# Gated cross-attention on one core: the instructions of a head in another order, with every step's place written out

## The reference

```python
def _L0_xattn_ref(latents, context, Wq, Wk, Wv, Wo, q_norm_w, k_norm_w):
    kv = jnp.concatenate([context, latents], axis=1)
    q = (latents @ Wq).reshape(bsz, q_len, HEADS, HEAD_DIM).transpose(0, 2, 1, 3)
    k = (kv @ Wk).reshape(bsz, kv_len, KV_HEADS, HEAD_DIM).transpose(0, 2, 1, 3)
    v = (kv @ Wv).reshape(bsz, kv_len, KV_HEADS, HEAD_DIM).transpose(0, 2, 1, 3)
    q = rms_norm(q, q_norm_w)
    k = rms_norm(k, k_norm_w)
    scores = jnp.einsum('bhgqd,bhkd->bhgqk', qg, k) * scale
    probs = jax.nn.softmax(scores.astype(jnp.float32), axis=-1).astype(q.dtype)
    out = jnp.einsum('bhgqk,bhkd->bhgqd', probs, v)
    return out @ Wo
x = x + jnp.tanh(g_xattn[0]) * _L0_xattn_ref(_layernorm(x), ctx_4096, ...)
x = x + jnp.tanh(g_ffn[0]) * _L0_ffn_ref(_layernorm(x), ...)
```

## Time and profile before

| what | before |
|---|---|
| median of 3 runs | 3681.51 us (3675.87 to 3684.28) |
| the profiled execution, its own time | 3666.57 us |
| its span in the profile | 3664.7 us |
| PE busy | 3162.6 us, 86% |
| DVE busy | 2476.6 us, 68% |
| ACT busy | 2036.9 us, 56% |
| POOL busy | 1343.4 us, 37% |
| mean granted TensorE clock | 0.955 |

### The profile page before, as it was taken

The page is one execution under the profiler, slowest core; times in us unless marked ns, Lnnn a source line. Parts: engine busy times, 40 slices in busy tenths (PEclk is TensorE's granted clock), DMA queues, the critical chain, the costliest instruction groups (busy, mean ns, idle before and its releaser), DMA issues. The chain is left out here.

```text
span 3664.7 us, 52293 instructions
## 1 busy us (share of the span) xinstructions
PE 3162.6 (86%) x14906; PEld 2518.2 (69%) x14906; DVE 2476.6 (68%) x3316; ACT 2036.9 (56%) x2899; POOL 1343.4 (37%) x791
## 2 busy tenths in 40 slices
PE   7978888888888888888888888888888888599699
PEld 5856677767667677766677776767776777377477
DVE  6854767777857777777677777676777677632666
ACT  3435666666656666665566666666666666431211
POOL 2321444444524444444244444443444444400000
PEclk9989999999999999999999999999999999799799
DMA  7870000000210000102000100020100000243410
GB/s 241 262 232 30 30 29 29 29 29 29 68 39 29 29 29 31 34 23 80 24 29 31 34 29 29 23 79 27 35 29 29 29 29 18 81 149 97 148 35 18
DMA packets 183908, 210.88 MB, mean 58 GB/s; under 512 B 10964, under 2 KB 125652, under 8 KB 182760
## 3 DMA queue, kind: packets, MB, share of 16 engines
q1 hardware_dynamic: 179016, 196.27, 16.6%
q0 software_dynamic: 2176, 8.39, 0.7%
q10 hardware_dynamic: 2592, 4.72, 0.4%
HBM read 140.14 MB, written 69.21 MB: 57 GB/s over the span
## 5 line engine op out<-in xcount | busy, mean ns | idle before, releaser
L745 ACT ACTIVATE att_sc<-att_pqk,att_rk 128x512 f32<-128x512 f32 (+1 forms) x960 | 661.8, 689 | 865.6 <-PE att_pqk L653 844.2
L867 POOL TENSOR_TENSOR att_sm<-att_sm,att_sc 128x1024 f32<-128x1024 f32 (+1 forms) x384 | 849.4, 2212 | 754.3 <-DVE att_pr L818 753.3
L673 PE MATMUL att_ppv<-att_pr,att_V 128*128 128x512 f32 (+1 forms) x2880 | 896.0, 421 | 127.9 <-ACT att_oraw L760 85.4
L653 PE MATMUL att_pqk<-att_q,att_kT 128*128 128x512 f32 (+1 forms) x2880 | 855.0, 407 | 7.9 <-issue 5.9
L614 PE MATMUL att_pkv<-att_ctxT,att_wkv 128*128 128x512 f32 (+1 forms) x3072 | 772.0, 384 | 102.5 <-DVE att_V L847 102.3
L614 PEld LDWEIGHTS att_pkv<-att_ctxT,att_wkv 128*128 128x128 f32 x3072 | 565.2, 193 | 234.4 <-DVE att_V L847 113.0
L673 PEld LDWEIGHTS att_ppv<-att_pr,att_V 128*128 128x128 f32 (+1 forms) x2880 | 524.9, 196 | 259.9 <-ACT att_oraw L760 103.4
L818 DVE TENSOR_TENSOR att_pr<-att_sc,att_pr 128x1024 fp32r<-128x1024 f32 (+1 forms) x512 | 628.1, 1227 | 109.0 <-ACT att_pr L756 108.7
L801 DVE TENSOR_TENSOR att_pmx<-att_pmx,att_sc 128x512 f32<-128x512 f32 x768 | 533.0, 694 | 237.8 <-ACT att_sc L745 232.6
L653 PEld LDWEIGHTS att_pqk<-att_q,att_kT 128*128 128x128 f32 (+1 forms) x2880 | 542.0, 191 | 146.4 <-ACT att_sc L745 8.1
L812 DVE TENSOR_TENSOR att_sc<-att_sc,att_pmax 128x1024 f32<-128x1024 f32 (+1 forms) x512 | 584.6, 1142 | 0.0
(11 more groups left out here) (130 smaller groups left out, 2738.4 us busy)
## 6 DMA issues: line engine op xcount, KB each, us to landing
q_scr<-pre_qT SPq DMA_DIRECT2D x128, 256.0 KB, 3.6
att_wkv<-kv_scr SPq DMA_DIRECT2D x64, 512.0 KB, 4.1
att_q<-q_scr SPq DMA_DIRECT2D x64, 512.0 KB, 4.1
o_scr<-att_on SPq DMA_DIRECT2D x64, 256.0 KB, 2.0
out_oraw<-o_scr SPq DMA_DIRECT2D x64, 256.0 KB, 4.6
att_sc<-in_ctx SPq DMA_DIRECT2D x16, 768.0 KB, 4.7
pre_wq_raw<-in_L_xattn_Wq SPq DMA_DIRECT2D x8, 1024.0 KB, 7.0
kv_scr<-pre_kv SPq DMA_DIRECT2D x8, 1024.0 KB, 7.5
```

Source lines behind the costliest of these rows:

```text
L653: mm = pe.matmul(pqk[0:m, (h * NT + t) % 2], kT[:, kp, t * P:t * P + m], q[:, qp, h], start=(i == 0), stop=(i == 2))
L673: mm = pe.matmul(ppv[:], V[0:m, vp, t], pr[0:m, pp, (t // 2) % NP, t % 2], start=(t == 0 and i == 0), stop=(t == NT - 1 and i == 2))
L745: act.activation(sc[0:m, h, t], pqk[0:m, s % 2], ACT.Copy, scale=rk[0:m, t:t + 1]).then_inc(sc_ok, 1)
L867: pool.tensor_tensor(sm[0:m, 0:w], sm[0:m, 0:w], sc[0:m, h, i:i + w], ALU.add).then_inc(sum_ok, w)
```

## The change

The step list gets a new form: the distances between steps, which were formulas (`p - 4.3`, `e + 1.59`, `k + i * 0.82`), become a table in which every kind of step has a place, for the two halves and for each chunk of keys and values apart. No step is added or removed, and no instruction, wait or buffer in the steps is changed. Lines after the table stand 3 lower than before.

```diff
--- before.py
+++ after.py
@@ -433,34 +433,37 @@
 
 
         LAG = 24
-        steps = []
+        TILE = dict(copy=0.39, pv=24.2, sub=19.6, exp=20.8, hi=21.6, lo=22.5, sum=23.0, max=1.78)
+        END = dict(mt=(2.49, 2.89),
+                   red=(2.9, 3.1),
+                   mb=(4.7, 5.1),
+                   oraw=(23.2, 23.2),
+                   fold=(23.8, 22.5),
+                   dt=(24.77, 24.07),
+                   dred=(25.03, 24.73),
+                   db=(26.66, 27.36),
+                   on=(30.31, 45.01),
+                   st=(28.31, 28.31),
+                   ldq=(-29.9, -29.9))
+        CHUNK = (dict(k=(-11.56, -11.5, -11.28), v=(1.44, 1.92, 2.0), khi=-11.46, klo=-9.93, kn=-6.16, var=-6.26, pow=-7.26, vhi=2.74, vt=12.5, vthi=13.36, vtlo=16.04),
+                 dict(k=(-7.48, -7.26, -6.8), v=(3.2, 7.72, 9.42), khi=-7.06, klo=-6.93, kn=-1.36, var=-2.36, pow=1.34, vhi=9.74, vt=16.8, vthi=17.26, vtlo=16.94),
+                 dict(k=(-5.79, -5.21, -4.47), v=(9.44, 13.2, 14.34), khi=-4.27, klo=-2.84, kn=0.23, var=-0.67, pow=5.33, vhi=15.24, vt=21.3, vthi=21.06, vtlo=21.64),
+                 dict(k=(-1.08, -0.66, -0.4), v=(17.82, 19.2, 19.34), khi=-0.06, klo=-0.63, kn=1.84, var=4.24, pow=8.84, vhi=19.74, vt=26.5, vthi=26.06, vtlo=27.24))
+        LOADS = dict(ldwk=-31.6, ldwv=-16.8)
+        steps = [(place, what, 0, 0) for what, place in LOADS.items()]
         for h in range(NH):
             for t in range(NT):
                 p = h * NT + t
-                steps += [(p, "qk", h, t), (p + 0.39, "copy", h, t), (p + LAG, "pv", h, t)]
+                steps += [(p, "qk", h, t), (p + TILE["copy"], "copy", h, t), (p + TILE["pv"], "pv", h, t)]
+                if t >= 1:
+                    steps += [(p + TILE["max"], "max", h, t)]
             for g, (t, z) in enumerate(GR):
-                p = h * NT + t + LAG
-                steps += [(p - 4.3, "sub", h, g), (p - 3.2, "exp", h, g), (p - 2.4, "hi", h, g), (p - 1.6, "lo", h, g)]
-                if g >= 1:
-                    steps += [(p - 0.9, "sum", h, g)]
-            for t in range(1, NT):
-                steps += [(h * NT + t + 1.18, "max", h, t)]
-            e = (h + 1) * NT
-            steps += [(e + 1.59, "mt", h, 0), (e + 1.7, "red", h, 0), (e + 3, "mb", h, 0)]
-            f = e + LAG
-            steps += [(f - 0.6, "oraw", h, 0), (f - 0.5, "fold", h, 0), (f + 1.17, "dt", h, 0), (f + 1.83, "dred", h, 0),
-                      (f + 3.76, "db", h, 0), (f + 4.21, "on", h, 0), (f + 4.31, "st", h, 0)]
-            steps += [(h * NT - NT + .1, "ldq", h, 0)]
-
-        for c, (k, v, vt) in enumerate(((-12.7, 1, 12.6), (-9, 6, 16.6), (-3.21, 13, 20.6), (-1.5, 17.5, 24.6))):
-            for i in range(PARTS):
-                steps += [(k + i * 0.82, "k", i, c), (v + i * 0.82, "v", i, c)]
-            k, v = k + (PARTS - 1) * 0.82, v + (PARTS - 1) * 0.82
-            steps += [(k + 0.9, "khi", 0, c), (k + 1.03, "klo", 0, c), (k + 3.5, "kn", 0, c),
-                      (k + 3.6, "var", 0, c), (k + 3.7, "pow", 0, c)]
-            steps += [(v + 0.9, "vhi", 0, c)]
-            steps += [(vt, "vt", 0, c), (vt + 0.76, "vthi", 0, c), (vt + 1.64, "vtlo", 0, c)]
-        steps += [(-28, "ldwk", 0, 0), (-10.4, "ldwv", 0, 0)]
+                p = h * NT + t
+                steps += [(p + TILE[what], what, h, g) for what in ("sub", "exp", "hi", "lo", "sum") if g >= 1 or what != "sum"]
+            steps += [((h + 1) * NT + place[h], what, h, 0) for what, place in END.items()]
+        for c, places in enumerate(CHUNK):
+            for what, place in places.items():
+                steps += [(p, what, i, c) for i, p in enumerate(place)] if what in ("k", "v") else [(place, what, 0, c)]
         steps.sort()
```

## The result

The changed kernel takes 3226.81 us (median of 4 runs, 3225.14 to 3228.32), the kernel before 3680.64 (4 runs, 3675.87 to 3684.28). The ratio is 0.8768, with a 95% interval of 0.8752 to 0.8783. The forecast was 3340, its range 3290 to 3460: the sign and the cause held, the gain was a third larger than foreseen, and the time lies 63 us under the range.

The account below looks back on a forecast made before the run. PE was taken as the bound: 74.67 us of work plus 10.63 of waits a round. Terms of -286, -29, -20 and -6 sum to -341; from the median 3681.5 that gives 3340 us, range 3290 to 3460.

Parts of the forecast that it names:

- the sign: Whole kernel: faster by more than 0.2%, about 8 us; chance 0.94, against 0.02 for within and 0.04 for slower.
- the cause: PE in the rounds: its waits behind chains just begun on PE go, about 0.45 us of 10.63 staying.
- the eight waits: PE waits in a steady round, for `sub`, `vhi`, `oraw` (twice), `vtlo` (twice), `klo` and `lo`: 10.63 us in all.
- The one foreseen to stay: `pv` of the next half waiting for `oraw`, with `exp` ahead on ACT: 0.45 us left a round.
- 24 rounds: Steady rounds of the four stretches: 75.5 us each, 1812 in place of 2097.75 us, so -286.
- The clock term: Half-clock spells in the 24 rounds, taken as gone with the waits; worth 50 us if all stayed.
- Last and first rounds and boundaries: Rest of each batch's last round -29, first rounds -20, three boundaries -6 us.
- the four waits of the earlier trace: PE waits in the first round of each batch, 7.1 us; 5 taken as going, -20 over the batches.
- The row that spoke against the change: `lo` between two batches held by POOL's `sum`, 2.56 against 1.221 us; expected holds of a few tenths, within margins.
- Rival 1: DVE becomes the bound: 14 full `lo` a round each held 2.40 us, +238 over 28 rounds, 3920 us; chance 0.04.
- Rival 2: New waits replace old ones as covers of 0.6 to 1 us are thin; half the gain lost, 3511; chance 0.16.
- Rival 3: PE's waits only moved: the same 10 us at other steps, 3680 us; chance 0.02.

## Why the prediction was right or wrong

**The cause was right.** Seven of the eight waits went, and each part taken back brings its own waits again: `oraw` those of `pv` for `oraw`, the `mb` part that for `sub` (and a new one of `mt`), the chunk places those for `vtlo`, `vhi` and `klo`. The one foreseen to stay, of `pv` for `oraw`, stayed, at 0.18 instead of 0.45. The chain behind it can be read on ACT:

```profile
1212.70 1.05 ACT L753 ACTIVATE att_sc<-att_sc 128x1024 f32<-128x1024 f32 x1
1213.65 0.57 ACT L763 COPY att_oraw<-att_ppv 128x512 f32<-128x512 f32 x1
1214.11 0.70 ACT L748 ACTIVATE att_sc<-att_pqk,att_rk 128x512 f32<-128x512 f32 x1
```

`oraw` began at 1213.65, 1.09 us after its `pv` (1212.56; the forecast took 1.12), behind the `exp`.

**The step that failed** is "It adds and removes nothing, so PE's 74.67 us of work stay, and only the waits can move", and with it the lower bound of 74.7 us "(no wait at all)". The busy time held a restart of about 0.29 us for each of the eight waits. A round without a wait takes 72.38. A second term was put at nothing: the half-clock spells outside the 24 rounds, worth about 20 us (below). The rows for the first were on the table: in the earlier trace rows the steps start 0.70 us apart and are shown 0.86 or 0.87 long, and in the earlier trace rows the same `pv` is 0.97 long behind a wait. The 0.16 us of overlap and the 0.10 us of growth are the price of a wait beyond its idle time, and I read past both.

By terms:

- *24 rounds,* -286 forecast, -344.7 measured. A round at clock 1.00 fell by 85.34 - 72.84 = 12.50 us instead of 9.84. Of the 2.66 between, seven restarts fewer make 7 x 0.29 = 2.03; the 0.4 us I had allowed for what I could not see was not needed, and the last wait was 0.27 shorter, together 2.70. Over 24 rounds that is 24 x 2.66 = 64. The clock term, 50 us, came whole: the four stretches now run at 1.00. It shows as 344.7 - 24 x 12.50 = 45, because the first distance of each stretch is 74.05 us instead of 72.84, 4.9 us in all; on PE's own marks that first round takes 73.35.
- *Last and first rounds and boundaries,* -55 forecast, -87.7 measured. In the parts of `attend` outside the four stretches, up to the last `qk`, PE waited 134.0 us in 95 pieces before and waits 75.8 in 65 pieces now: 58 us less, near the forecast by sum, though the four waits of the earlier trace rows fell from 7.1 to 0.7 us (I had taken 5) and the wait of `mb` in that round, 1.4 us, which I had not counted, went too. Thirty restarts fewer make 9 us. The other 21 fit the clock, for which I had no term here: by the records of the granted clock it was at half for 110.5 us in these parts and is for 66.3 now, and in the 24 rounds 106.9 us at half had cost the 50. One such part, around the first boundary, before and after:

```profile
897.02:1097.10 200.08, 168.40 (x792) 132.57 (x791) 139.24 (x176) 121.04 (x173) 80.23 (x44) 0.94 0.15 49
820.24:996.19 175.95, 159.56 (x787) 127.26 (x786) 135.57 (x175) 121.65 (x173) 78.58 (x43) 0.97 0.17 56
```

- *Behind the last `qk`,* 0 forecast, -8.4 measured; 2.3 of it up to the last `db`. The other 6 lie in stages that the change doesn't touch. The clock is at half for 6.6 us less there, which can be worth half of that; the rest stays unexplained.
- *The level of the median.* I carried over that the median lay 14.9 us above the profiled execution. After, it lies 1.0 above. That difference belonged to the one profiled execution of before and should have gone into the range. The 0.2% that I called no change was too small as well: the later runs of the kernel before spread over 1.1%.

The misses add up to 59 + 33 + 8 + 14 = 114 us, which is the way from 3340 to 3226.8. The lower end of the range shared the false bound of the round. With 72.84 in place of 74.7 it would have been 3290 - 45 = 3245, still 18 us too high: the restarts and the clock outside the 24 rounds were missing too.

**The row that spoke against the change** was read rightly: `lo` is held by some tenths, the sum bears it. The Trainium skill, SBUF — State Buffer, section "Who interferes with whom", has the one that comes second blocked until the first is done; the traces agree, with 2.54 us in place of 1.22 in the tail. Rival 1, DVE as the bound, fell: the held `lo` add 14 x 0.17 = 2.4 us to a round, not 33.6. Rival 2, half of the gain lost to new waits, fell: the 2.8 and 2.7 us of holds on DVE and ACT reach PE nowhere in the round. Its idea is sound, though, for a change made by halves: the parts done alone gave 277 us of 454, in part since new and longer waits took their place. Rival 3 fell by the result.

## What to carry to other kernels

Cost each wait of the bounding engine as its idle time plus a restart, and read the restart from two rows: how much a step's row overlaps the next one's start, and how much longer the step behind a wait is shown. Look for half-clock time in every part of the program whose waits change, not in the steady rounds alone. In a pipeline in a fixed order, waits share their slack: removing one moves the engine up against the next, so parts tried one at a time look poor, and a reordering is judged, and its gain summed, only with every chain moved at once. Count for each chain how much work of the bounding engine stands between its start and its use; that count foretold here which waits went and which one stayed.
